# Residual with a per-sample weight matrix on one core: later bias tiles made inside the groups, the load list first in the plan, early stores issued by GpSimd, ten row slots

## The chip, the cores and the metric

The kernel runs on one core of one Trainium2 chip. The metric is the device time of one execution in microseconds (us), as the median over runs. Engines are called TensorE (PE, with its weight loads PEld), VectorE (DVE), ScalarE (ACT), GpSimd (POOL) and SyncE (SP). The last one only issues transfers and waits.

## What is computed

```python
# x [128, 64, 256] f32, cat [128] int32 in 0..63, W [64, 256, 256] f32, b [64, 256] f32
selected_W = W[cat]
selected_b = b[cat]
out = x + jnp.einsum('bsd,bdh->bsh', x, selected_W) + selected_b[:, None, :]
```

The categories of the samples are drawn once from a fixed seed. Of 64 categories 54 occur. Counted in the order in which the 128 samples meet them, the groups of eight samples need, from the first group on, the first 8, 14, 20, 26, 32, 33, 38, 41, 44, 47, 48, 52, 53, 53, 53 and 54 of the weight matrices.

## The kernel before

**Tiling.** 128 samples are 16 groups of 8. A group is 4 pairs; two pairs are a quad and share one PSUM bank of `mm_ps` (4 banks). One weight matrix is 256 KB. `w_all` has room for all 64, in the order of first use. Rows of x (512 KB a group) lie in `rows`, which has X_SLOTS = 9 slots; the sum is added in place there and stored from there, so a load of group g + 9 waits for the stores of group g.

**Plan.** The order of loads is worked out on the chip. DVE and PE make from the categories a list of categories in order of first use (`load_words`, announced by `plan_read` 1) and the slot of each sample (`slot_words`, `plan_read` 2). The steps are counted in `plan_step`, the products in `plan_products`. DVE runs its steps in program order: `same` (L362) and `in_category` (L364) stand ahead of `has_place` (L372), which the list needs, and `place_powers` (L375) stands ahead of the copy of the list (L378).

**Bias.** The bias row of each sample comes from an f32 product of a one-hot matrix with the bias table (`bias_of_tile`, one for each of 4 tiles of 32 samples). DVE splits it into three bf16 parts (`split_bias`, five instructions), and for every pair PE first writes those parts to PSUM (L508). Tile 0 is made before the first transposes, tiles 1 to 3 right after the transposes of group 0 (L467 to L470). ACT then copies them to `bias_of` (L314, L315), and DVE splits tile t at the end of its loop over group t - 1.

**Group loop on PE.** `group(g)` transposes the rows of group g + 1 (L436, 8 matmuls), writes the bias parts (L508, 8) and then does 32 matmuls (L522), four at a time waiting in pairs of `w_slot` copies. DVE copies even weights from `w_all` to `w_slot` and ACT the odd ones (L281); each copy waits for the reports of loads (`w_loads_done`). DVE adds the sums to `rows` (L405).

**Loads and stores.** The first 8 matrices are loaded by SP and ACT (one before the list exists), all others by GpSimd in the order of the list, at most 8 in flight (L256). The rows of groups 2 to 15 are loaded by GpSimd too, after the loads named in `X_AFTER_LOAD`. GpSimd begins when REPORTED_FIRST = 3 loads are reported (L246), loads group 2's rows, then reads the first word of the list (L250). For every fourth load it reads a new word. Loads from the 40th on are made only if the list is that long; a load left out still takes its turn and is reported.
SP waits for the loads in order and reports each (L204). Between the reports it issues the stores of groups 0 to 6, after the report numbers of `STORE_AFTER_REPORTS` (14, 20, 27, 35, 43, 51, 59); the stores of groups 7 to 14 come behind the 64th report. A store of a group is two transfers of 256 KB (`store_quad`), each after a wait for its sum.

Of the kernel before, what the change touches and what calls it, by code (L numbers as in the profile page):

```python
# [14 lines left out]
PAIR = 2  # L15
X_SLOTS = 9
XT_SLOTS = 2
# [4 lines left out]
FIRST_LOADS = 8  # L22
REPORTED_FIRST = 3
CERTAIN_LOADS = 40
# [6 lines left out]

PLAN_STEPS = {"samples": 6, "first": 9, "bias": 13, "list": 14, "slots": 16}

X_AFTER_LOAD = {3: 13, 4: 19, 5: 24, 6: 29, 7: 33, 8: 37, 9: 40, 10: 43, 11: 46, 12: 48, 13: 50, 14: 55, 15: 60}
STORE_AFTER_REPORTS = {0: 14, 1: 20, 2: 27, 3: 35, 4: 43, 5: 51, 6: 59}


def build_cond_residual(nc, x, cat, weights, bias, out):  # L40
# [18 lines left out]
    assert FIRST_LOADS == PAIR * WORD  # L59
    assert all(at >= min(C, GROUP * (g + 1) + QUAD - 1) for g, at in STORE_AFTER_REPORTS.items())  # L60
    assert all(X_AFTER_LOAD[g + X_SLOTS] + 1 >= STORE_AFTER_REPORTS[g] for g in range(GROUPS - X_SLOTS))

# [4 lines left out]
    with ExitStack() as ctx:  # L67
# [38 lines left out]
        bias_parts = sb("bias_parts", [ROWS, TILES, H], BF16)  # L106
        bias_of = sb("bias_of", [ROWS, TILES - 1, H])
        bias_rest = sb("bias_rest", [ROWS, H])
# [14 lines left out]
        loads_ps = mm_ps[1][0:1, 0, LIST_WORDS:LIST_WORDS + 1]  # L123
        bias_ps = [mm_ps[r][0:ROWS, n, :] for r, n in ((2, 0), (1, 1), (3, 0), (3, 1))]

# [6 lines left out]
        plan_read = sem("plan_read")  # L132
        bias_copied = sem("bias_copied")
        bias_step = sem("bias_step")
# [4 lines left out]
        x_loaded = [sem(f"x_loaded{n}") for n in range(GROUPS)]  # L139
        stored = [sem(f"stored{n}") for n in range(X_SLOTS)]  # L140
        last_stored = sem("last_stored")
        halves_transposed = sem("halves_transposed")
# [39 lines left out]
        @block.sync  # L182
        def _(sp):
            sp.dma_start(cat_row_i[:, :], cat.partition_broadcast(P)).then_inc(cats_loaded, 16)
            load_rows(sp, 0)
            sp.dma_start(bias_nat[:, :], bias).then_inc(bias_loaded, 16)

            sp.wait_ge(cats_loaded, 32)
            for g in range(1, FIRST_X):
                load_rows(sp, g)  # L190

            sp.wait_ge(plan_read, 1)
            for n in range(1, FIRST_LOADS, PAIR):
                if n % WORD == 1:
                    word = words_read(mybir.EngineType.SP, load_words[0:1, n // WORD:n // WORD + 1],
                                      2 ** (WORD * BITS) - 1)[0]
                load_weights(sp, n, part(word, n % WORD))
            for n in range(C):

                if n < FIRST_LOADS:  # L200
                    sp.wait_ge(first_w_loaded[n], 16)
                else:
                    sp.wait_ge(w_loaded[n % LOADS_IN_FLIGHT], 16 * ((n - FIRST_LOADS) // LOADS_IN_FLIGHT + 1))
                sp.sem_inc(w_loads_done, 1)  # L204
                for g, after in STORE_AFTER_REPORTS.items():
                    if after == n + 1:
                        for q in range(QUADS_IN_GROUP * g, QUADS_IN_GROUP * (g + 1)):

                            sp.wait_ge(sums_added, q + 1)
                            store_quad(sp, q, stored[g % X_SLOTS])  # L210
            for q in range(QUADS_IN_GROUP * len(STORE_AFTER_REPORTS), last_group):

                sp.wait_ge(sums_added, q + 1)
                store_quad(sp, q, stored[q // QUADS_IN_GROUP % X_SLOTS])
            for p in range(0, PAIRS_IN_GROUP, PAIR):

                sp.wait_ge(sums_added, last_group + p + 1)
                store_pair(sp, p, last_stored)

            for g in range(GROUPS - X_SLOTS - 1, GROUPS - 1):  # L220
                sp.wait_ge(stored[g % X_SLOTS], stores_until(g))
            sp.wait_ge(last_stored, 16 * PAIRS_IN_GROUP)

        @block.gpsimd
        def _(pool):
# [15 lines left out]
            pool.iota(iota_part[:, :], [[0, 1]], base=0, channel_multiplier=1,  # L241
                      allow_small_or_imprecise_dtypes=True).then_inc(consts_ready, 1)

            pool.wait_ge(plan_read, 1)

            pool.wait_ge(w_loads_done, REPORTED_FIRST)  # L246
            load_rows(pool, FIRST_X)
            for n in range(FIRST_LOADS, C):
                if n % WORD == 0:
                    word = words_read(mybir.EngineType.Pool, load_words[0:1, n // WORD:n // WORD + 1],  # L250
                                      2 ** (WORD * BITS) - 1)[0]
# [10 lines left out]
                for g, after in X_AFTER_LOAD.items():  # L262
                    if after == n:
                        if g >= X_SLOTS:

                            pool.wait_ge(stored[g % X_SLOTS], stores_until(g - X_SLOTS))
                        load_rows(pool, g)

        def slots_of(engine, g, half):
# [15 lines left out]
        def _(act):  # L285
# [25 lines left out]
            slots = slots_of(mybir.EngineType.Activation, 0, 1)  # L311

            act.wait_ge(plan_products, 5)
            nc.scalar.copy(bias_of[:, 0, :], bias_ps[1]).then_inc(bias_copied, 1)  # L314
            nc.scalar.copy(bias_of[:, 1:TILES - 1, :], mm_ps[3][0:ROWS, :, :]).then_inc(bias_copied, 1)  # L315
            for g in range(GROUPS):
# [15 lines left out]
        def _(dve):  # L332
# [9 lines left out]
            for n in range(WORD):  # L342
# [18 lines left out]
            V.tensor_scalar(cat_powers[:, :], powers[:, :], cat_col[:, 0:1], None, ALU.mult).then_inc(plan_step, 1)  # L361
            V.tensor_scalar(same[:, :], cat_row_i[:, :], cat_col[:, 0:1], None, ALU.is_equal).then_inc(plan_step, 1)  # L362
            dve.wait_ge(consts_ready, 5)
            V.tensor_scalar(in_category[:, :, :, :], cat_row_i[0:C, :].rearrange("c (t n) -> c t n", n=TILE)  # L364
                            .unsqueeze(2).broadcast_to([C, TILES, SPLITS, TILE]),
                            iota_part[0:C, 0:1], None, ALU.is_equal).then_inc(plan_step, 1)
            steps[0] += 4
            assert steps[0] == PLAN_STEPS["bias"]


            dve.wait_ge(plan_products, 1)
            step(V.tensor_scalar(has_place[:, :], iota_far[:, :], place_ps, None, ALU.is_equal))  # L372
            assert steps[0] == PLAN_STEPS["list"]
            step(V.tensor_scalar(place[:, :], place_ps, FAR, first_here[:, 0:1], ALU.add, ALU.mult))
            step(V.tensor_scalar(place_powers[:, :], powers[:, :], place[:, 0:1], None, ALU.mult))  # L375
            assert steps[0] == PLAN_STEPS["slots"]
            dve.wait_ge(plan_products, 2)
            V.tensor_copy(load_words[:, :], mm_ps[1][0:1, 0, 0:LIST_WORDS + 1]).then_inc(plan_read, 1)  # L378
            dve.wait_ge(plan_products, 3)
            V.tensor_copy(slot_words[:, :], slot_words_ps).then_inc(plan_read, 1)  # L380
# [29 lines left out]
            for g in range(GROUPS - 1):  # L410

                now, slots = slots, slots_of(mybir.EngineType.DVE, g + 2, 0) if g + 2 < GROUPS else None
                for n in range(QUADS_IN_GROUP):
                    q = QUADS_IN_GROUP * g + n

                    dve.wait_ge(pairs_done, PAIR * (q + 1))
                    add_rows(rows[:, g % X_SLOTS, PAIR * n:PAIR * (n + 1), :], mm_ps[q % BANKS][:, :, :])
                    for p in range(PAIR * n, PAIR * n + PAIR):
                        copy_weights(dve, V.tensor_copy, now[p], g + 1, p, 0, even_weights_ready)
                if g + 1 < TILES:  # L420

                    dve.wait_ge(bias_copied, 2)
                    dve.wait_ge(bias_ready, PAIR * (g + 1))
                    split_bias(g + 1, bias_of[:, g, :])
            for p in range(PAIRS_IN_GROUP):
# [5 lines left out]
        def _(pe):  # L431
# [26 lines left out]
            last.then_inc(plan_products, 1)  # L458

            pe.wait_ge(bias_loaded, 16)  # L460
            bias_of_tile(0).then_inc(plan_products, 1)

            pe.wait_ge(x_loaded[0], 16)
            for k in range(K):
                transpose_half(0, k)

            pe.wait_ge(plan_read, 1)  # L467
            for t in range(1, TILES):
                last = bias_of_tile(t)
            last.then_inc(plan_products, 1)  # L470

            def group(g):
# [17 lines left out]

                pe.wait_ge(xT_ready, K * (g + 1))
                if g == 0:

                    pe.wait_ge(bias_ready, PAIR)

                    pe.wait_ge(bias_copied, 2)
                if PAIRS_IN_GROUP * g % PAIRS_IN_TILE == 0:

                    pe.wait_ge(bias_ready, PAIR * (PAIRS_IN_GROUP * g // PAIRS_IN_TILE + 1))
                for pair in range(PAIRS_IN_GROUP):  # L500
# [49 lines left out]
```

## Time and profile before

| what | value |
|---|---|
| median of 3 runs | 106.52 us (105.53 to 107.8) |
| profiled execution, its own time | 107.0 us |
| span of the profiled execution | 105.3 us |
| PE busy | 90.7 us (86% of the span) |
| DVE, ACT, GpSimd busy | 56.2, 56.3, 45.8 us |
| moved by DMA | 31.26 MB, 297 GB/s over the span |

The span runs from the first to the last instruction. Busy time is time with an instruction in work on that engine. A share of the span is an average over stages with different limits, so the stages have to be looked at one by one. The granted clock of TensorE is given as a share of full speed (2.4 GHz), so 0.5 is 1.2 GHz. The DMA share is the mean busy share of the 16 DMA engines.

### The profile page before, as it was taken

How to read it: one execution, taken by the hardware profiler on the slowest of the kernel's cores; microseconds unless marked ns; L12 is line 12 of the kernel's file. 1: busy time of each engine (PE TensorE's matmuls, PEld its weight loads, DVE VectorE, ACT ScalarE, POOL GpSimd, SP SyncE). 2: the span in 40 equal slices, each digit the busy share in tenths (PEclk: the TensorE clock that was granted, in tenths of full speed). 3: DMA queues.
4: the chain of work that ended last, by engine and by line, in shares of the span. 5: the costliest groups of instructions: out<-in, count | busy, mean ns of one | idle time of the engine just before them, and what ended most of it. 6: DMA issues, size and time to landing. Idle time of an engine off the chain costs nothing.

```text
span 105.3 us, 3045 instructions
## 1 busy us (share of the span) xinstructions
PE 90.7 (86%) x786; PEld 60.5 (57%) x786; DVE 56.2 (53%) x137; ACT 56.3 (53%) x99; POOL 45.8 (43%) x81
## 2 busy tenths in 40 slices
PE   0039999999958838999999999999999999999960
PEld 0026576656626517557576767666766767676630
DVE  1086403558848696175547473829282828364740
ACT  0000866556324618279766666667585858584400
POOL 5000078977888889867678353005503011000000
PEclk9999999999999998599999999999999999999999
DMA  0576998999999999999999999926883805999994
GB/s 10 150 266 170 345 340 274 356 325 339 377 396 351 389 402 361 353 401 387 364 363 398 406 361 375 403 90 120 254 332 120 280 11 184 330 343 326 305 344 168
DMA packets 18049, 31.26 MB, mean 297 GB/s; under 512 B 1840, under 2 KB 13296, under 8 KB 18032
## 3 DMA queue, kind: packets, MB, share of 16 engines
q0 software_dynamic: 5696, 19.40, 51.5%
q1 hardware_dynamic: 10816, 10.36, 29.3%
q10 hardware_dynamic: 1520, 1.31, 4.4%
q8 instruction: 6, 0.10, 0.4%
q14 instruction: 11, 0.09, 0.2%
HBM read 25.30 MB, written 8.39 MB: 320 GB/s over the span
## 4 chain that ended last, share of the span: by engine, by line
PE 59%; DMA 14%; issue 11%; POOLq 4%; POOL 4%; DVE 3%; ACT 1%; SPq 1%; ACTq 0%
PE mm_ps L522 39%; PE xt_ps L436 11%; DMA w_all<-in_L_cond_W 10%; PE mm_ps L508 6%; DMA cat_col_i<-in_itok_B 4%; POOL w_all L159 3%; POOLq L153 2%; POOLq L159 2%; PE xt_ps L522 2%; POOL rows L168 1%; ACT w_slot L281 1%; DVE rows L405 0%; DVE same_ahead L354 0%; SPq L153 0%; DVE in_category L364 0%
## 5 line engine op out<-in xcount | busy, mean ns | idle before, releaser
L522 PE MATMUL mm_ps<-w_slot,xT 128*64 128x256 f32 x496 | 58.5, 385 | 4.0 <-ACT w_slot L281 3.9
L281 ACT COPY w_slot<-w_all 128x512 f32 x64 | 39.0, 620 | 31.4 <-SPq L204 16.5
L522 PEld LDWEIGHTS mm_ps<-w_slot,xT 128*64 128x64 f32 x496 | 35.4, 140 | 22.0 <-issue 6.2
L159 POOL DMA_DIRECT2D w_all<-in_L_cond_W x56 | 33.2, 595 | 14.8 <-issue 7.3
L405 DVE TENSOR_TENSOR rows<-mm_ps,rows 128x512 f32<-128x512 f32 (+1 forms) x32 | 21.5, 673 | 25.3 <-PE mm_ps L522 24.5
L281 DVE COPY w_slot<-w_all 128x512 f32 x64 | 26.7, 446 | 13.4 <-SPq L204 13.3
L168 POOL DMA_DIRECT2D rows<-in_x x14 | 10.9, 781 | 26.4 <-DMA out<-rows 16.1
L436 PE MATMUL xt_ps<-ident,rows 128*128 128x128 f32 x128 | 19.9, 304 | 0.1
L436 PEld LDWEIGHTS xt_ps<-ident,rows 128*128 128x128 f32 x128 | 15.6, 154 | 7.0 <-issue 6.0
L293 ACT COPY xT<-xt_ps 128x512 f32<-128x512 f32 x32 | 17.1, 584 | 0.0
L508 PE MATMUL mm_ps<-bias_parts,is_sample 96*64 96x256 bf16 x124 | 10.8, 297 | 0.0
L508 PEld LDWEIGHTS mm_ps<-bias_parts,is_sample 96*64 96x64 bf16 x124 | 6.0, 115 | 3.1 <-issue 2.8
L293 ACT ACT_TABLE_LOAD x1 | 1.3, 1283 | 10.6 <-issue 10.6
L447 PE MATMUL mm_ps<-is_first,ahead_or_self 128*128 128x1 bf16 x1 | 0.2, 183 | 5.8 <-DVE is_first L357 5.8
L442 PE MATMUL mm_ps<-bias_nat,in_category 64*96 64x256 f32 x8 | 4.0, 658 | 0.0
L447 PEld LDWEIGHTS mm_ps<-is_first,ahead_or_self 128*128 128x128 bf16 x1 | 0.1, 102 | 5.8 <-DVE is_first L357 5.8
L442 PEld LDWEIGHTS mm_ps<-bias_nat,in_category 64*96 64x96 f32 x8 | 1.9, 268 | 1.0 <-issue 0.3
L522 PE MATMUL xt_ps<-w_slot,xT 128*64 128x256 f32 x16 | 2.1, 379 | 0.0
L351 DVE CAST cat_col<-cat_col_i 128x1 f32<-128x1 int32 x1 | 0.2, 155 | 3.1 <-DMA cat_col_i<-in_itok_B 3.1
L398 DVE TENSOR_TENSOR bias_parts<-bias_rest,bias_mid 32x256 bf16<-32x256 f32 x4 | 1.7, 417 | 0.1
L522 PEld LDWEIGHTS xt_ps<-w_slot,xT 128*64 128x64 f32 x16 | 1.1, 137 | 0.6
L395 DVE TENSOR_TENSOR bias_rest<-bias_of,bias_parts 96x256 f32<-96x256 f32 x3 | 1.3, 422 | 0.1
(42 smaller groups left out, 13.1 us busy)
## 6 DMA issues: line engine op xcount, KB each, us to landing
w_all<-in_L_cond_W POOLq DMA_DIRECT2D x56, 256.0 KB
out<-rows SPq DMA_DIRECT2D x30, 256.0 KB, 4.1
rows<-in_x POOLq DMA_DIRECT2D x14, 512.0 KB, 7.6
rows<-in_x SPq DMA_DIRECT2D x2, 512.0 KB, 4.6
w_all<-in_L_cond_W ACTq DMA_DIRECT2D x4, 256.0 KB, 4.8
w_all<-in_L_cond_W SPq DMA_DIRECT2D x4, 256.0 KB, 6.1
out<-rows SPq DMA_DIRECT2D x2, 128.0 KB, 2.9
out<-rows ACTq DMA_DIRECT2D x2, 128.0 KB, 2.9
```

What stands on the lines that cost most here:

```text
L153: return nc.values_load_multi_w_load_instructions(words, engines=[engine], min_val=0, max_val=most)[1]
L159: engine.dma_start(w_all[:, n, :, :], weights[bass.ds(c, 1), :, :].rearrange("c (k p) h -> p (c k) h", p=P), **how).then_inc(first_w_loade ...
L168: engine.dma_start(rows[:, g % X_SLOTS, :, :], x_groups[g]).then_inc(x_loaded[g], 16)
L281: copy(w_slot[:, PAIR * p + half, :, :].rearrange("p k h -> p (k h)"), w_all[:, bass.ds(c, 1), :, :].rearrange("p c k h -> p (c k h)")).th ...
L293: nc.scalar.copy(xT[:, slot, k].rearrange("p j s -> p (j s)"), xt_ps[slot][k][:, :, :].rearrange("p t r -> p (t r)")).then_inc(xT_ready, 1)
L395: split(V.tensor_tensor(bias_rest[all3, :], whole, bias_parts[all3, t, :], ALU.subtract))
L398: V.tensor_tensor(bias_parts[third, t, :], bias_rest[third, :], bias_mid[third, :], ALU.subtract).then_inc(bias_ready, 1)
L405: V.tensor_tensor(to, sums, to, ALU.add).then_inc(sums_added, 1)
L436: last = T.transpose(xt_ps[g % XT_SLOTS][k][:, p, :], rows[:, g % X_SLOTS, p, k * P:(k + 1) * P], ident[:, :])
L442: return T.matmul(bias_ps[t], in_category[:, t, :, :].rearrange("c a n -> c (a n)"), bias_nat[:, :], start=True, stop=True)
L508: T.matmul(sums(pair)[HALF * half:HALF * (half + 1), :], is_sample[:, sample + half:sample + half + 1].broadcast_to([ROWS, HALF]), bias_pa ...
L522: last = T.matmul(to[HALF * half:HALF * (half + 1), :], xT[:, slot, k, j, :], w_slot[:, j, k, :], start=False, stop=(k == K - 1), skip_gro ...
```

## The change

`PLAN_STEPS` is put into a new order: DVE makes `has_place`, `place` and the copy of the list before `same`, `place_powers` and `in_category`. Tiles 1 to 3 of the bias are no longer made ahead of group 0: PE makes tile g in `group(g)`, behind its transposes, in a bank of `mm_ps` that has just come free, and DVE splits it straight from PSUM at the start of its loop over group g. The copies on ACT and `bias_of` are gone. GpSimd reads its first list word before it waits for the reports, and waits for five of them, not three. GpSimd also issues the stores of groups 0 to 10: those of groups 0 to 6 behind loads 33, 37, 40, 43, 46, 51 and 59, the rest after its last load. SP stores groups 11 to 15. There are ten row slots.

```diff
-X_SLOTS = 9
+X_SLOTS = 10
-REPORTED_FIRST = 3
+REPORTED_FIRST = 5
-PLAN_STEPS = {"samples": 6, "first": 9, "bias": 13, "list": 14, "slots": 16}
+PLAN_STEPS = {"samples": 6, "first": 9, "list": 12, "slots": 15, "bias": 16}
-X_AFTER_LOAD = {3: 13, 4: 19, 5: 24, 6: 29, 7: 33, 8: 37, 9: 40, 10: 43, 11: 46, 12: 48, 13: 50, 14: 55, 15: 60}
-STORE_AFTER_REPORTS = {0: 14, 1: 20, 2: 27, 3: 35, 4: 43, 5: 51, 6: 59}
+X_AFTER_LOAD = {3: 13, 4: 19, 5: 24, 6: 29, 7: 33, 8: 37, 9: 40, 10: 43, 11: 46, 12: 48, 13: 51, 14: 55, 15: 60}
+STORE_AFTER_LOAD = {0: 33, 1: 37, 2: 40, 3: 43, 4: 46, 5: 51, 6: 59}
+POOL_GROUPS = 11
...
-        bias_ps = [mm_ps[r][0:ROWS, n, :] for r, n in ((2, 0), (1, 1), (3, 0), (3, 1))]
+        bias_ps = [mm_ps[r % BANKS][0:ROWS, 0, :] for r in (2, 4, 6, 8)]
...
 # SP
-                for g, after in STORE_AFTER_REPORTS.items():
-                    if after == n + 1:
-                        for q in range(QUADS_IN_GROUP * g, QUADS_IN_GROUP * (g + 1)):
-                            sp.wait_ge(sums_added, q + 1)
-                            store_quad(sp, q, stored[g % X_SLOTS])
-            for q in range(QUADS_IN_GROUP * len(STORE_AFTER_REPORTS), last_group):
+            for q in range(QUADS_IN_GROUP * POOL_GROUPS, last_group):
                 sp.wait_ge(sums_added, q + 1)
-                store_quad(sp, q, stored[q // QUADS_IN_GROUP % X_SLOTS])
+                store_quad(sp, q, late_stored)
...
 # GpSimd
+            def store_group(g):
+                for q in range(QUADS_IN_GROUP * g, QUADS_IN_GROUP * (g + 1)):
+                    pool.wait_ge(sums_added, q + 1)
+                    store_quad(pool, q, stored[g % X_SLOTS])
             pool.wait_ge(plan_read, 1)
+            word = words_read(mybir.EngineType.Pool, load_words[0:1, FIRST_LOADS // WORD:FIRST_LOADS // WORD + 1],
+                              2 ** (WORD * BITS) - 1)[0]
             pool.wait_ge(w_loads_done, REPORTED_FIRST)
             load_rows(pool, FIRST_X)
...
+                for g, after in STORE_AFTER_LOAD.items():
+                    if after == n:
+                        store_group(g)
+            for g in range(len(STORE_AFTER_LOAD), POOL_GROUPS):
+                store_group(g)
...
 # ACT
-            act.wait_ge(plan_products, 5)
-            nc.scalar.copy(bias_of[:, 0, :], bias_ps[1]).then_inc(bias_copied, 1)
-            nc.scalar.copy(bias_of[:, 1:TILES - 1, :], mm_ps[3][0:ROWS, :, :]).then_inc(bias_copied, 1)
...
 # DVE, in its loop over g
+                if 1 <= g < TILES:
+                    dve.wait_ge(tiles_made, g)
+                    dve.wait_ge(bias_ready, PAIR * g)
+                    split_bias(g, bias_ps[g])
                 for n in range(QUADS_IN_GROUP):
...
-                if g + 1 < TILES:
-                    dve.wait_ge(bias_copied, 2)
-                    dve.wait_ge(bias_ready, PAIR * (g + 1))
-                    split_bias(g + 1, bias_of[:, g, :])
...
 # PE
-            pe.wait_ge(plan_read, 1)
-            for t in range(1, TILES):
-                last = bias_of_tile(t)
-            last.then_inc(plan_products, 1)
...
                 pe.wait_ge(xT_ready, K * (g + 1))
+                if 1 <= g < TILES:
+                    pe.wait_ge(sums_added, QUADS_IN_GROUP * (g - 1) + 1)
+                    bias_of_tile(g).then_inc(tiles_made, 1)
                 if g == 0:
                     pe.wait_ge(bias_ready, PAIR)
-                    pe.wait_ge(bias_copied, 2)
-                if PAIRS_IN_GROUP * g % PAIRS_IN_TILE == 0:
-                    pe.wait_ge(bias_ready, PAIR * (PAIRS_IN_GROUP * g // PAIRS_IN_TILE + 1))
+                elif 1 < g <= TILES:
+                    pe.wait_ge(bias_ready, PAIR * g)
```

## Rows read from the trace of the kernel before

**Rows 1.** Page, part 2: granted TensorE clock in 40 equal slices, in tenths.

```profile
PEclk9999999999999998599999999999999999999999
```

**Rows 2.** Chain that ended last, in order of time: start us, us, what.

```profile
31.68 7.19 DMA w_all<-in_L_cond_W
...
47.52 1.03 PE xt_ps L436 x8
48.54 0.56 PE mm_ps L508 x8
49.10 3.46 PE mm_ps L522 x32
```

**Rows 3.** Timeline of PE, 25 to 48 us: start, us, instruction, [idle before <-releaser].

```profile
31.93 1.08 PE L522 MATMUL mm_ps<-w_slot,xT 128*64 128x256 f32 x8 [1.52 <-ACT w_slot L281]
...
39.77 1.08 PE L522 MATMUL mm_ps<-w_slot,xT 128*64 128x256 f32 x8 [1.87 <-ACT w_slot L281]
...
43.28 4.23 PE L522 MATMUL mm_ps<-w_slot,xT 128*64 128x256 f32 x32
```

**Rows 4.** Busy time by stretch: PE, PEld, DVE, ACT, POOL, PEclk, DMA share, GB/s.

```profile
24.00:38.90 14.90, 11.64 (x103) 7.47 (x99) 11.10 (x27) 6.04 (x11) 12.19 (x18) 1.00 1.03 376
...
30.00:40.80 10.80, 6.91 (x61) 4.32 (x57) 7.91 (x19) 5.13 (x10) 9.09 (x13) 1.00 1.04 382
40.80:44.60 3.80, 3.80 (x26) 2.79 (x26) 1.43 (x4) 1.46 (x3) 3.46 (x6) 0.55 1.02 347
```

**Rows 5.** Reports of loads (L204), six stretches from 0: count, ns, first to last.

```profile
L204 SPq EVENT_SEMAPHORE  x3: 17/17/17, 11.9 to 12.3; - x3
...
L204 SPq EVENT_SEMAPHORE  x5: 17/17/17, 11.9 to 15.6; - x5
...
L204 SPq EVENT_SEMAPHORE  x8: 17/17/17, 11.9 to 17.6; - x8
...
L204 SPq EVENT_SEMAPHORE  x26: 17/17/17, 11.9 to 38.9; - x26
...
L204 SPq EVENT_SEMAPHORE  x32: 17/17/17, 11.9 to 45.3; - x32
...
L204 SPq EVENT_SEMAPHORE  x47: 17/17/17, 11.9 to 64.7; - x47
```

**Rows 6.** Timeline of GpSimd, 12 to 46 us.

```profile
13.01 0.89 POOL L168 DMA_DIRECT2D rows<-in_x  x1 [10.24 <-SPq L204]
14.54 2.86 POOL L159 DMA_DIRECT2D w_all<-in_L_cond_W  x4 [0.64 <-issue]
17.91 1.43 POOL L159 DMA_DIRECT2D w_all<-in_L_cond_W  x2 [0.51 <-issue]
```

**Rows 7.** Timeline of all engines, 0 to 22 us: plan and bias tiles.

```profile
6.53 0.25 DVE L372 TENSOR_SCALAR has_place<-iota_far,mm_ps 128x64 bf16<-128x64 f32 x1
...
7.32 0.17 DVE L378 CAST load_words<-mm_ps 1x17 int32<-1x17 f32 x1
...
10.55 2.87 PE L442 MATMUL mm_ps<-bias_nat,in_category 64*96 64x256 f32 x6
```

**Rows 8.** Issues by line, stores in two stretches: count, ns, first to last; landing.

```profile
L159 POOL DMA_DIRECT2D w_all<-in_L_cond_W x56: 44/706/795, 14.5 to 88.0; - x56
...
DMA to landing us min/median/max: 3.2/6.0/6.2
...
L168 POOL DMA_DIRECT2D rows<-in_x x14: 748/776/892, 13.0 to 86.4; - x14
...
L172 SPq DMA_DIRECT2D out<-rows x2: 393/448/502, 23.5 to 23.9; - x2
...
L172 SPq DMA_DIRECT2D out<-rows x2: 373/422/472, 31.1 to 31.5; - x2
...
DMA to landing us min/median/max: 7.0/8.3/9.7
```

**Rows 9.** Waits, longest first: us in total, times, longest us.

```profile
POOL rows L168 <- DMA out<-rows: 16.1, 4, 7.1
```

More of the change, by code:

```diff
@@ L59, in build_cond_residual @@
     assert FIRST_LOADS == PAIR * WORD
-    assert all(at >= min(C, GROUP * (g + 1) + QUAD - 1) for g, at in STORE_AFTER_REPORTS.items())
-    assert all(X_AFTER_LOAD[g + X_SLOTS] + 1 >= STORE_AFTER_REPORTS[g] for g in range(GROUPS - X_SLOTS))
+    assert all(at + 1 >= min(C, GROUP * (g + 1) + QUAD - 1) for g, at in STORE_AFTER_LOAD.items())
+    assert all(X_AFTER_LOAD[g + X_SLOTS] >= STORE_AFTER_LOAD[g] for g in range(GROUPS - X_SLOTS))
     x_groups = x.rearrange("(g p h) s d -> g (h s) p d", p=PAIRS_IN_GROUP, h=PAIR)
@@ L106, in build_cond_residual @@
         bias_parts = sb("bias_parts", [ROWS, TILES, H], BF16)
-        bias_of = sb("bias_of", [ROWS, TILES - 1, H])
         bias_rest = sb("bias_rest", [ROWS, H])
@@ L132, in build_cond_residual @@
         plan_read = sem("plan_read")
-        bias_copied = sem("bias_copied")
+        tiles_made = sem("tiles_made")
         bias_step = sem("bias_step")
@@ L140, in build_cond_residual @@
         stored = [sem(f"stored{n}") for n in range(X_SLOTS)]
+        late_stored = sem("late_stored")
         last_stored = sem("last_stored")
@@ L218, in _ @@
                 store_pair(sp, p, last_stored)
-            for g in range(GROUPS - X_SLOTS - 1, GROUPS - 1):
+            for g in range(POOL_GROUPS - X_SLOTS, POOL_GROUPS):
                 sp.wait_ge(stored[g % X_SLOTS], stores_until(g))
+            sp.wait_ge(late_stored, 16 * (last_group - QUADS_IN_GROUP * POOL_GROUPS))
             sp.wait_ge(last_stored, 16 * PAIRS_IN_GROUP)
@@ L248, in _ @@
             for n in range(FIRST_LOADS, C):
-                if n % WORD == 0:
+                if n % WORD == 0 and n > FIRST_LOADS:
                     word = words_read(mybir.EngineType.Pool, load_words[0:1, n // WORD:n // WORD + 1],
@@ L361, in _ @@
             V.tensor_scalar(cat_powers[:, :], powers[:, :], cat_col[:, 0:1], None, ALU.mult).then_inc(plan_step, 1)
-            V.tensor_scalar(same[:, :], cat_row_i[:, :], cat_col[:, 0:1], None, ALU.is_equal).then_inc(plan_step, 1)
+            steps[0] += 2
             dve.wait_ge(consts_ready, 5)
[L364 to L368, printed above, removed]
             dve.wait_ge(plan_products, 1)
@@ L374, in _ @@
             step(V.tensor_scalar(place[:, :], place_ps, FAR, first_here[:, 0:1], ALU.add, ALU.mult))
-            step(V.tensor_scalar(place_powers[:, :], powers[:, :], place[:, 0:1], None, ALU.mult))
-            assert steps[0] == PLAN_STEPS["slots"]
             dve.wait_ge(plan_products, 2)
             V.tensor_copy(load_words[:, :], mm_ps[1][0:1, 0, 0:LIST_WORDS + 1]).then_inc(plan_read, 1)
+            V.tensor_scalar(same[:, :], cat_row_i[:, :], cat_col[:, 0:1], None, ALU.is_equal).then_inc(plan_step, 1)
+            V.tensor_scalar(place_powers[:, :], powers[:, :], place[:, 0:1], None, ALU.mult).then_inc(plan_step, 1)
+            steps[0] += 2
+            assert steps[0] == PLAN_STEPS["slots"]
+            V.tensor_scalar(in_category[:, :, :, :], cat_row_i[0:C, :].rearrange("c (t n) -> c t n", n=TILE)
+                            .unsqueeze(2).broadcast_to([C, TILES, SPLITS, TILE]),
+                            iota_part[0:C, 0:1], None, ALU.is_equal).then_inc(plan_step, 1)
+            steps[0] += 1
+            assert steps[0] == PLAN_STEPS["bias"]
             dve.wait_ge(plan_products, 3)
@@ L458, in _ @@
             last.then_inc(plan_products, 1)
+            pe.wait_ge(plan_step, PLAN_STEPS["bias"])
             pe.wait_ge(bias_loaded, 16)
```

## The prediction

> **What bounds the kernel now.** Read the clock by slices first, then the chain of work that ended last, then the idle times on PE's timeline. The chain shows two regimes. From about 40.9 us to the end it lies on PE, in groups that repeat: 1.03 us of transposes, 0.56 of bias parts, 3.46 of products, 5.05 us together [rows 2]. Nothing waits there. Before that, the chain runs along GpSimd's issues and ends in the landing of the 26th weight load: issued at 31.68, landed 7.19 us later [rows 2]. The report comes at 38.9 [rows 5], ACT copies the matrix, and PE's last eight products of group 3 start at 39.77 after 1.87 us of idleness; in group 2 the same place had 1.52 us [rows 3]. From 30 to 40.8 us PE is busy for 6.91 of 10.80 us, while the DMA engines are full (share 1.04, 382 GB/s) [rows 4]. So groups 1 to 3 are paced by the supply of weights, groups 4 to 15 by PE. After that poor stretch the clock falls: its mean is 0.55 from 40.8 to 44.6 [rows 4], and the dip to 0.8 and 0.5 is the only one in the slices [rows 1]. That is the lower level, 1.2 GHz, for most of the stretch, and group 4 lasts from 40.85 (39.77 + 1.08) to 47.52 [rows 2, 3], 6.67 us and not 5.05: 1.6 us lost.
>
> Hence the rule for this case: what moves the end of group 4 moves the end of the kernel one for one, if the later weights keep ahead of PE. What does not is hidden.
>
> **The stores moved behind the weights.** The stores of group 0 (two transfers at 23.5 and 23.9) and group 1 (31.1 and 31.5) share the full DMA engines with loads 15 to 26 [rows 8]. The latter pair lands up to 9.7 us after its issue, to 41.2, so of the four transfers of 0.262 MB about 3.5 are moved before 38.9: 0.92 MB. At 376 GB/s, the rate from 24 to 38.9 us [rows 4], that is 2.4 us. The changed kernel issues its first store after the 34th load, so report 26 gains these 2.4 us as far as the transfers set it.
>
> **The list earlier.** `has_place` starts at 6.53 because it stands behind `in_category`; the copy of the list starts at 7.32, behind `place_powers` [rows 7]. With those behind it, `has_place` can start when `in_category` would have, some 0.4 us sooner, and the list gains about 0.15 us more since `place_powers` no longer stands ahead of its copy: 0.55 us. The bounds are 0.2 and the 0.8 us between the two starts. The first eight loads start that much earlier. The slots and bias tile 0 come 0.1 to 0.2 us later; hidden, since group 0 waits for weights.
>
> **GpSimd starts later.** Three reports are there at 12.3, five at 15.6, all eight at 17.6 [rows 5]. GpSimd's rows load, now queued behind the fifth report, was issued at 13.01, 0.7 us after the third, and its first weights at 14.54 [rows 6]. In the changed kernel the fifth report comes earlier: 0.55 us for the list, and about 0.65 us because the 0.52 MB of rows issued at 13.01 no longer share the engines then (about 0.2 MB of it by 15.6, at the rate above). That is 14.4. The word of the list is already read, so the first weights follow 0.7 + 0.9 us after: 16.0, 1.4 us later than now. Bounds: 0, if the fifth report came right behind the third, and 2.1 us with no relief but the list's (15.6 - 0.55 + 1.6 - 14.54). Everything GpSimd issues is behind this wait: the rows of group 2, then all loads.
>
> GpSimd's own pace then matters. From its first weights to the 26th load (index 25) there are 17 loads of 0.706 us (12.0), three rows loads of 0.776 (2.3) [rows 8] and four word reads at 0.5 [rows 6] (2.0): 16.3 us, where it took 17.1 now (31.68 - 14.54). So the 26th load is issued at 32.4, 0.7 later than now. Landing: a load takes 3.2 us at least, 6.0 in the median, this one 7.19 [rows 2, 8]. With no store between I take 4.3, near the lower end, since the eight first loads are through before GpSimd's come: report 26 at 36.7 (35.6 to 38.4). By the transfers: 38.9 - 2.4 - 0.55, and plus about 1.0 us for a gap in the DMA stream while GpSimd waits, gives 36.95. The two ways agree; I take 36.7, **2.2 us earlier**.
>
> **Group 4.** From report 26 to the end of group 3 it takes 2.0 us now (38.9 to 40.85 [rows 3, 5]), so group 3 ends at 38.7. Report 32 follows after six loads and one rows load, 2.1 MB, 5.6 us at 376 GB/s: 42.3 (45.3 now, with stores in between [rows 5]). Its copy and products put the end of group 4 at 44.3 or later; PE alone would need 38.7 + 5.05 = 43.75 at full clock. So 44.3 against 47.52: **3.2 us**. The clock's 1.6 us is in this, with 0.55 us of it spent on the wait for report 32. I count the clock as staying at 2.4 GHz since PE's idleness in groups 2 and 3 shrinks: each group has now about 6.4 us for 5.5 us of work, where it was busy for 64% of the stretch from 30 to 40.8.
>
> **The bias tiles.** Three tiles took PE 2.87 us at the low clock ahead of group 1's transposes [rows 7]. They go to groups 1 to 3, 0.96 us each at the low and about 0.48 at the full clock. In groups 1 to 3 the last weights are later than PE's other work, so 0.5 us a group is covered (without the cover, were PE to bound there, 1.4 us in all). Group 0 gets the 2.87 us back, but weights and clock pace it: counted 0. DVE now waits in groups 1 to 3 for PE's tile before it can split; behind that wait stand the sum of the group's first quad and the even copies of the next group, which are not due for some 3 us. PE's next user of that sum is two groups on: 0. ACT loses two copies, ahead of odd weights that mostly have not landed: 0 to 0.3 us, I take 0.
>
> **Stores on GpSimd.** No row shows a store issued there. The nearest below is the same transfer on SP (0.37 to 0.50 us to issue), the nearest above the same 256 KB as a load on GpSimd, 0.706, at most 0.795, and a rows load at up to 0.892 [rows 8]. I take 0.71, the same size and row length. Eight of them (groups 0 to 3) stand ahead of the 47th load: 5.7 us. By issue alone, from 32.4 on with 21 loads (14.8), five rows loads (3.9), five word reads (2.5) and these, the 47th goes out at 32.4 + 26.9 = 59.3 and lands by 63.6; by transfers, 21 loads, five rows loads and four groups of stores after report 26, 10.2 MB at 376 GB/s, it is 27.2 us after 36.7: report 47 at 63.9, 64.7 now [rows 5]. Group 9, whose last pair needs it, ends near 44.3 + 5 x 5.05 = 69.6, and wants the report by 67.6. So 3.7 us to spare, and more for the other groups. Each such store also waits for its sum, with loads queued behind it; the sums are long there (group 3's at about 39, its store near 56).
>
> The Trainium skill, page "SBUF — State Buffer", section "SBUF: two separate sides", has a rule that speaks against this edit: DVE's f32 copies inside SBUF lock GpSimd out while it makes descriptors. It gives 620 ns alone and 3100 ns beside such a copy, by which the eight stores would cost up to 20 us more. This trace does not agree: of 56 issues, with DVE's even copies running between them, none took over 795 ns [rows 8]. The sum goes by that row.
>
> **Ten slots, SP at the end.** GpSimd waits 16.1 us in four places for stores before rows loads [rows 9]; these are off the chain. With ten slots and the stores queued well ahead the waits go; what becomes free is time on GpSimd, worth nothing at the end. The stores of groups 7 to 10 leave before the tail, so the last stores meet emptier engines: 0 to 0.3 us, I take 0.1.
>
> **Sum.** 3.2 + 0.1 = 3.3 us. 107.0 - 3.3 = 103.7 for the profiled execution; the median shown is 0.5 us lower than that execution, so **103.2 us**.
>
> **The rivals.**
> 1. *The clock falls all the same*, or stays at the low level through group 1. For it: gaps in groups 2 and 3 remain. Against it: they are halved. Cost 1.6 less the 0.55 us that group 4 waits anyway: 1.0, so 104.2. Chance 0.13.
> 2. *Issue, not transfer, sets the supply.* If landing stays at the 6.0 median or more, report 26 comes at 38.4 or later, and little is gained: the chain of before does run along GpSimd from 13 to 31.7 us, and it now starts later. Against it: engines full at 1.04. Time 105.3 to 106.5, say 105.9. Chance 0.13.
> 3. *More is gained*: with earlier first weights and no stores, PE bounds from group 0 on. It can't end group 4 before about 19 + 3 x 5.5 + 5.05 = 40.6, a gain of 6.9 (19 is my estimate for the end of group 0: eighth report at 17.6 - 0.55 - 1.2, plus 3 us for the last two pairs at the low clock). Time 99.6 to 101.7, say 101.2. Chance 0.10.
> 4. *Slower: stores issued by GpSimd make later weights late.* The 3.7 us to spare at load 47 are gone in transfers; on the issue side (63.6 against 67.6) eight stores may each cost 0.5 us more, 1.21 us. Beyond that point each further 0.1 us costs 0.8 us, and the gain of 3.3 is used up at 1.6 us a store. At 2.0 us each: 103.2 + 8 x (2.0 - 1.21) = 109.5, slower than before. The lock named above would work so. Against it: the 795 ns. Chance 0.05.
>
> **How the numbers follow.** The forecast holds 0.59, its own range 101.9 to 104.4 (report 26 from 35.8 to 38.0). With rivals 1 and 3 in part and 2 in part, 101.0 to 105.6 leaves out 0.2: half of rivals 2 and 3, rival 4 and a little more. About 2% can be told from no change, so faster is under 104.4: the forecast nearly whole (0.56), rival 3 (0.10), over half of rival 1 (0.08): 0.74. Within 2%: 0.21. Slower: 0.05.
>
> **What would show it.** Right: no store before load 34; report 26 between 36 and 37.5; clock 1.0 from 36 to 46 us; group 4 over by 44.5; from there groups of 5.05; GpSimd's stores at 0.7 us; no wait for `out` before rows loads. Wrong: the first GpSimd weights after 16.7, a store over 1.2 us, groups past the fourth longer than 5.1 us, or a wait of PE for rows of group 2, issued 2 us later than now.

## The result, and the profile after

| kernel | median us | ratio to the kernel before | 95% interval |
|---|---|---|---|
| before | 106.59 | 1 | |
| changed | 105.37 | 0.9882 | 0.9846 to 0.9919 |

The change takes 1.2 us off, not 3.3. The time lies within the range that was given, near its upper end; the gain is about a third of the forecast. A second measurement gave less still: a ratio of 0.994 (0.990 to 0.999). Here and below the medians count every execution, while the ratios leave out the slow ones, those over 1.5% longer than the fastest of their kernel, of which the profiled execution of the kernel before with five reports is one (110.82 us). The profiled execution of the changed kernel took 105.33 us with a span of 103.6, so its span is 1.7 us shorter. I follow these 1.7 us.

First the granted clock and the flow of data by slices, page, part 2, of the changed kernel:

```profile
PEclk9999999999999999999999999999999999999999
DMA  0587994999999999999999999999997799993353
GB/s 10 143 273 220 291 314 167 334 324 331 354 332 350 353 347 345 348 356 399 351 391 372 394 367 400 373 388 350 373 392 271 227 333 320 331 322 114 108 202 105
```

The dip of the clock [rows 1] is gone. But two things stand in the GB/s row: a hole (167) at 15.5 to 18 us, with a DMA share of 0.4, and then a flat stretch near 350 up to 44 us, where the kernel before had 376 to 382 up to 40.8 us [rows 4] with stores among its loads.

The reports of loads (L207 of the changed kernel), counted from 0, answer to [rows 5]:

```profile
L207 SPq EVENT_SEMAPHORE  x5: 17/17/17, 11.3 to 14.8; - x5
...
L207 SPq EVENT_SEMAPHORE  x14: 17/17/17, 11.3 to 24.9; - x14
...
L207 SPq EVENT_SEMAPHORE  x26: 17/17/17, 11.3 to 38.6; - x26
...
L207 SPq EVENT_SEMAPHORE  x32: 17/17/17, 11.3 to 44.6; - x32
...
L207 SPq EVENT_SEMAPHORE  x64: 17/17/17, 11.3 to 81.0; - x64
```

Of the kernel before, these are the two that [rows 5] does not have:

```profile
L204 SPq EVENT_SEMAPHORE  x14: 17/17/17, 11.9 to 23.4; - x14
...
L204 SPq EVENT_SEMAPHORE  x64: 17/17/17, 11.9 to 88.0; - x64
```

Report 14 is 1.5 us later than before, report 26 only 0.3 us earlier and report 32 0.7 us. So the supply lost 1.5 us at its start, won it back, and won hardly more. The timeline of GpSimd answers to [rows 6]:

```profile
15.13 0.90 POOL L171 DMA_DIRECT2D rows<-in_x  x1 [12.37 <-SPq L207]
16.03 2.82 POOL L162 DMA_DIRECT2D w_all<-in_L_cond_W  x4
...
32.12 2.11 POOL L162 DMA_DIRECT2D w_all<-in_L_cond_W  x3
```

The 26th load (index 25) is the first of the three from 32.12 on. The timeline of PE answers to [rows 3]:

```profile
28.86 0.64 PE L450 MATMUL mm_ps<-bias_nat,in_category 64*96 64x256 f32 x2 [0.79 <-DVE rows L413]
...
39.48 1.08 PE L527 MATMUL mm_ps<-w_slot,xT 128*64 128x256 f32 x8 [1.20 <-ACT w_slot L292]
...
45.51 1.08 PE L527 MATMUL mm_ps<-w_slot,xT 128*64 128x256 f32 x8 [0.76 <-ACT w_slot L292]
```

In the chain that ended last, the landing from which it passes to PE is now that of the 32nd load:

```profile
37.38 7.22 DMA w_all<-in_L_cond_W
```

Group 4 ends at 46.59 (45.51 + 1.08) and not at 47.52, 0.93 us earlier. It runs at full clock, and part of what the clock gives back it spends waiting for its last weights (0.76 us). From there the groups take 5.04 us each, as before, and the last sum comes 0.93 us earlier too. The remaining 0.8 us of the span are at the very end. The last stores of pairs, from issue to landing, in the kernel before and then in the changed one:

```profile
DMA to landing us min/median/max: 2.6/2.9/3.3
```

```profile
DMA to landing us min/median/max: 1.7/1.7/1.8
```

### The profile page after: what moved, and what is told of

The parts are those of the page before. It is cut to its first block, busy times and chain, and to the rows that moved or that the text cites. A ratio compares the mean times of both kernels' runs of the same rounds, so it can differ in the third digit from the quotient of the medians.

```text
span 103.6 us, 3047 instructions
## 1 busy us (share of the span) xinstructions
PE 87.4 (84%) x786; PEld 58.2 (56%) x786; DVE 57.0 (55%) x137; ACT 55.0 (53%) x97; POOL 62.0 (60%) x103
## 3 DMA queue, kind: packets, MB, share of 16 engines
q1 hardware_dynamic: 4832, 4.59, 13.5%
## 4 chain that ended last, share of the span: by engine, by line
PE 54%; DMA 16%; issue 15%; POOL 6%; POOLq 3%; DVE 2%; ACT 1%; ACTq 0%; SPq 0%; DVEq 0%
PE mm_ps L527 36%; DMA w_all<-in_L_cond_W 12%; PE xt_ps L444 10%; PE mm_ps L513 6%; POOL w_all L162 5%; DMA cat_col_i<-in_itok_B 4%; POOLq L162 2%; PE xt_ps L527 2%; POOL rows L171 1%; POOLq L156 1%; ACT w_slot L292 1%; DVE rows L413 0%; DVE same_ahead L361 0%; DVE has_place L373 0%; PE mm_ps L458 0%
## 5 line engine op out<-in xcount | busy, mean ns | idle before, releaser
L527 PE MATMUL mm_ps<-w_slot,xT 128*64 128x256 f32 x496 | 57.8, 380 | 5.3 <-ACT w_slot L292 4.0
L527 PEld LDWEIGHTS mm_ps<-w_slot,xT 128*64 128x64 f32 x496 | 34.5, 137 | 22.9 <-issue 4.9
L413 DVE TENSOR_TENSOR rows<-mm_ps,rows 128x512 f32<-128x512 f32 (+1 forms) x32 | 21.6, 674 | 23.9 <-PE mm_ps L527 23.0
L444 PE MATMUL xt_ps<-ident,rows 128*128 128x128 f32 x128 | 19.0, 298 | 0.4 <-DMA rows<-in_x 0.4
L171 POOL DMA_DIRECT2D rows<-in_x x14 | 11.0, 786 | 13.5 <-SPq L207 12.9
L175 POOL DMA_DIRECT2D out<-rows x22 | 16.1, 736 | 1.1 <-issue 1.1
L513 PE MATMUL mm_ps<-bias_parts,is_sample 96*64 96x256 bf16 x124 | 9.9, 278 | 0.1
L450 PE MATMUL mm_ps<-bias_nat,in_category 64*96 64x256 f32 x8 | 3.1, 478 | 0.8 <-DVE rows L413 0.8
L402 DVE CAST bias_parts<-mm_ps 96x256 bf16<-96x256 f32 x4 | 1.7, 420 | 1.9 <-PE mm_ps L450 1.0
L450 PEld LDWEIGHTS mm_ps<-bias_nat,in_category 64*96 64x96 f32 x8 | 1.1, 182 | 1.5 <-issue 1.3
L403 DVE TENSOR_TENSOR bias_rest<-mm_ps,bias_parts 96x256 f32<-96x256 f32 x4 | 1.7, 420 | 0.1
```

The source lines that it names most:

```text
L171: engine.dma_start(rows[:, g % X_SLOTS, :, :], x_groups[g]).then_inc(x_loaded[g], 16)
L175: engine.dma_start(out_pairs[:, PAIR * q:PAIR * (q + 1), :], rows[:, g % X_SLOTS, PAIR * n:PAIR * (n + 1), :]).then_inc(done, 16)
L402: split(V.tensor_copy(bias_parts[all3, t, :], whole))
L403: split(V.tensor_tensor(bias_rest[all3, :], whole, bias_parts[all3, t, :], ALU.subtract))
L413: V.tensor_tensor(to, sums, to, ALU.add).then_inc(sums_added, 1)
L444: last = T.transpose(xt_ps[g % XT_SLOTS][k][:, p, :], rows[:, g % X_SLOTS, p, k * P:(k + 1) * P], ident[:, :])
```

## The experiments

All ratios are to the kernel before as run in the same comparison; there were four (106.59, 106.60, 106.13 and 106.41 us). "Group 4 ends" is the start of group 5's transposes in the chain of the profile, or the end of group 4's products on PE's timeline. The row "before, five reports" comes from an execution 1.7 us longer than the median of its kernel, so its three times are too late by an unknown part of that.

| run | median us | ratio, 95% interval | report 14 | report 26 | group 4 ends |
|---|---|---|---|---|---|
| before | 106.59 | 1 | 23.4 | 38.9 | 47.5 |
| before, five reports | 109.14 | 1.022 (1.016 to 1.028) | 26.3 | 42.9 | 51.5 |
| before, no early stores | 104.47 | 0.979 (0.972 to 0.985) | 23.1 | 37.9 | 45.8 |
| before, ten slots | 105.97 | 0.999 (0.995 to 1.003) | 23.6 | 39.5 | 48.1 |
| changed | 105.37 | 0.988 (0.985 to 0.992) | 24.9 | 38.6 | 46.6 |
| changed, again | 106.11 | 0.994 (0.990 to 0.999) | 24.8 | 39.3 | 47.3 |
| changed, all stores on SP | 107.02 | 1.006 (1.002 to 1.010) | 23.9 | 39.5 | 47.8 |
| changed, three reports | 103.76 | 0.973 (0.969 to 0.977) | 23.5 | 37.9 | 45.9 |
| the same, again | 103.96 | 0.980 (0.975 to 0.985) | 23.3 | 37.4 | 45.4 |
| changed, one report | 104.32 | 0.984 (0.980 to 0.989) | 23.2 | 37.0 | 44.9 |
| changed, three reports, all stores on SP | 105.74 | 0.995 (0.991 to 1.000) | 23.3 | 38.3 | 46.9 |
| changed, stores of 7 to 10 on SP | 105.95 | 0.997 (0.993 to 1.001) | 24.4 | 38.3 | 46.3 |
| changed, rows on SP | 109.39 | 1.032 (1.026 to 1.039) | 26.0 | 38.4 | 46.0 |
| the same, three reports | 109.60 | 1.031 (1.022 to 1.039) | 24.2 | 36.7 | 49.2 |

Two profiles of an unaltered kernel differ here by 0.7 us at report 26, so single profiles are read in pairs where that can be done.

### What the early stores cost the loads

```diff
 # the kernel before; x of groups 9 and 10 wait for the sums instead
-                    if after == n + 1:
+                    if after == n + 1 and g > 1:
```

> The kernel before, with the stores of groups 0 and 1 left out altogether (their part of the output is not written). It measures what these four transfers of 0.262 MB cost the loads. Theory 'part price': loads alone run at 349 GB/s and stores beside them raise the total, so a stored byte costs the loads only about 0.6 of a byte: report 26 at 38.9 - 1.8 = 37.1 us. Rival 'full price' (that of my prediction): 1.05 MB at 349 GB/s, report 26 at 35.9 to 36.5. Rival 'free': report 26 stays at 38.9. Of the time, part price gives 1.5 to 3 us less than the kernel before, full price 3 to 4, free none.

Report 26 came at 37.9, 1.0 us earlier. That is between free and part price: 1.05 MB at 349 GB/s would be 3.0 us, so a stored byte costs the loads about a third of a byte at report 26. By the bytes loaded it is more: from 24 to 38.9 us this kernel loaded 5.12 MB and the kernel before 4.56, which is 0.56 MB for 1.03 MB of stores. Part of that went to loads behind the 26th. The time fell by 2.1%, within the 1.5 to 3 us; group 4 ended 1.7 us earlier, more than report 26 moved, since the clock stayed up (PE's row of the clock has no dip) and report 32 came 1.4 us earlier.

The reason can be read from the busy time by stretch, 25 to 38 us. Columns are as in [rows 4]. The kernel before, with stores; then without the early ones; then the changed kernel:

```profile
25.00:38.00 13.00, 10.64 (x94) 6.69 (x90) 9.34 (x23) 5.04 (x9) 10.54 (x16) 1.00 1.04 378
```

```profile
25.00:38.00 13.00, 10.93 (x98) 7.01 (x94) 9.68 (x23) 4.68 (x9) 11.77 (x17) 1.00 1.01 347
```

```profile
25.00:38.00 13.00, 12.11 (x108) 8.03 (x108) 11.04 (x25) 6.55 (x12) 12.12 (x17) 1.00 1.02 349
```

The engines are full in all three (1.01 to 1.04). Loads alone move 347 and 349 GB/s in these 13 us, and 346 to 353 in the other kernels without early stores. With stores among them it is 378, and 368 to 377 in three of the four other kernels that store there; the fourth, the kernel before with five reports, stored half as much in the stretch (0.52 MB) and had 350. The DMA queues of the stretch from 24 to 38.9 us split this: packets, MB, share of the engines. First the kernel before, then the changed one:

```profile
q0 software_dynamic: 1358, 4.56, 82.8%
q1 hardware_dynamic: 1060, 1.03, 19.8%
```

```profile
q0 software_dynamic: 1539, 5.19, 101.6%
```

In 14.9 us the kernel before loaded 4.56 MB and stored 1.03 beside it; the changed one loaded 5.19. Taking 1.03 MB of stores away brought 0.63 MB of loads here. So a busy share of 1.0 did not mean that a byte taken away frees its whole time.

### Is it reads that are limited, or GpSimd's queue?

```diff
 # the changed kernel; SP, behind its report
+                for g, after in X_AFTER_LOAD.items():
+                    if max(after - LOADS_IN_FLIGHT + 1, 0) == n:
+                        if g >= X_SLOTS:
+                            sp.wait_ge(stored[g % X_SLOTS], stores_until(g - X_SLOTS))
+                        load_rows(sp, g)
 # GpSimd
-                        load_rows(pool, g)
```

> The changed kernel with the rows loads of groups 3 to 15 issued by SP in its report loop, as the reports of eight loads earlier come. It asks why loads alone stay at 349 GB/s. Theory 'read limit': reads are limited whatever queue they come from, so the total stays at 340 to 355 GB/s from 25 to 38 us and report 26 near 38.6. Rival 'queue limit': GpSimd's queue alone can't do more; with a quarter of the bytes on SP's queue the total rises to 376 or more, report 26 comes 1 us earlier, and the time falls by 1 us or more.

The same stretch of that kernel, then its two queues from 25 to 38 us:

```profile
25.00:38.00 13.00, 11.87 (x106) 7.70 (x104) 9.97 (x24) 7.07 (x13) 9.66 (x14) 1.00 1.05 349
```

```profile
q0 software_dynamic: 1066, 3.48, 78.6%
q1 hardware_dynamic: 1030, 1.03, 25.3%
```

Here too q1 carries 1.03 MB beside q0 (in the kernel before these were stores), and the total is 349, not 376. The changed kernel shows the other half. Its stores begin at 41 us on GpSimd's own queue, so that one queue carries loads and stores together, and from 44.6 us on the rate is higher:

```profile
44.60:60.00 15.40, 14.64 (x140) 9.97 (x140) 8.86 (x18) 11.96 (x22) 14.72 (x21) 1.00 1.03 377
```

So it is the direction and not the queue: over long stretches loads alone stay near 349 GB/s here, and stores beside them raise the sum. Nor is it GpSimd's issuing: with three reports it was busy for 10.87 and 10.70 of the 13 us, and not for 12.12, at the same 348 and 349 GB/s. The figure is no hard stop over a short time: from 15 to 20 us, with the last of the first eight loads still arriving, the two runs with three reports loaded at 355 and 363 GB/s. Why loads alone stay there was not found. Report 26 came at 38.4, as the read limit has it. The time was not the same, though: it is 3% above the kernel before and some 4% above the changed one, and all of that comes after group 4. The rows now share the engines with the weights on a queue of their own and come late (issue to landing 11.5 us in the median, 7.6 in the changed kernel). PE idled 3.6 us for them in five places, 0.4 us in the changed kernel, which is about the 3.3 us by which the span is longer:

```profile
PE xt_ps L443 <- DMA rows<-in_x: 3.6, 5, 1.0
```

> As the run with rows loads on SP, with GpSimd's start behind three reports. Read limit: the time of the changed kernel with three reports, 103.8 us, within 0.5 us. Queue limit: 102.5 to 103.0 us.

It gave 348 GB/s from 25 to 38 us and 109.6 us. The rate held, the time did not. PE idled 4.7 us for rows, 2.1 of them at 35.15 us, and here the clock fell as well, to 0.6 and 0.5 of full speed from 35 to 43 us.

### GpSimd's later start

```diff
-REPORTED_FIRST = 5
+REPORTED_FIRST = 3
```

> The changed kernel with GpSimd's start behind three reports as before instead of five. Theory 'late start': the five-report wait costs the supply 1.1 us or more, at report 14 (24.9 in the changed kernel, 23.4 before) and still at report 26: expect report 14 at 23.2 to 23.8, report 26 at 37.3, and 1.0 to 1.4 us less than the changed kernel. Rival 'caught up': loads in flight catch up by report 26; 38.6 as now, and the same time. Rival 'first loads first': the rows load in front of the first eight delays report 8 by 0.8 us and the time is not better.

> The changed kernel once more, unaltered, for a comparison on one chip with the runs with three and one reports: 105.2 to 105.5 us if the kernel before gives 106.5.

> The changed kernel with three reports once more, on the same chip as the changed kernel: 1.2 to 1.6 us less than it if the earlier comparison (0.9727 against 0.9882 of the kernel before) holds, 0.7 us less if the profile's spans (102.9 and 103.6) tell the truth.

On one chip, three reports gave 103.96 and five 106.11; in the separate comparisons 103.76 and 105.37. In ratios that is 1.4 to 1.6% or 1.5 to 1.7 us. Over two profiles each, report 14 comes at 23.4 and not 24.9, report 26 at 37.7 and not 39.0, group 4 ends at 45.7 and not 47.0: what is lost at the start is still missing at group 4. "Caught up" and "first loads first" are out (report 8 comes 0.2 to 0.4 us later, not 0.8, and the time is better). The gain is somewhat above the 1.0 to 1.4 us expected, and the changed kernel's second time is above its 105.2 to 105.5. The stretch from 15 to 20 us shows the hole and its absence, the changed kernel first, then with three reports:

```profile
15.00:20.00 5.00, 3.75 (x31) 2.56 (x32) 1.78 (x3) 3.06 (x6) 4.49 (x7) 1.00 0.70 226
```

```profile
15.00:20.00 5.00, 3.94 (x32) 2.69 (x32) 2.23 (x4) 3.21 (x6) 4.62 (x7) 1.00 1.04 355
```

The 26th load shows what binds. With three reports it was issued at 30.26 and 30.40 and not at 32.12, and landed only 0.7 and 1.2 us earlier, after 7.7 and 7.0 us and not after 6.5. Issued earlier, it waits longer.

As for the hole, 129 GB/s over 5 us are 0.65 MB, or 1.8 us at 349 GB/s; 0.2 MB of it had been moved earlier, from 10 to 15 us (311 against 272 GB/s).

> The kernel before with GpSimd's start behind five reports instead of three, nothing else. Late start: report 14 from 23.4 to 25, report 26 from 38.9 to about 40, time 1.0 to 1.5 us more than the kernel before. Caught up: report 26 and the time as before.

In the kernel before, the same single number costs 2.3 to 2.5 us (1.022), against 1.0 to 1.5 expected. Report 14 is 2.9 us later in its profiled execution, but that one was 1.7 us longer than the median. There GpSimd also reads its first word only behind the wait, the clock falls again, and the stores keep their places. How much each of these adds was not taken apart.

> The changed kernel with GpSimd's start behind one report. Late start goes on: one report is there at 11.3, some 0.9 us before the third; if the start sets the supply, report 26 comes near 37.0 and the time falls another 0.5 to 0.9 us below the one with three reports. Rival 'engines full': from 10 us on the engines are busy at 0.91 and more with three reports, so nothing is gained, and the first eight weights come up to 0.8 us later: the same time or up to 0.5 us more.

Report 26 moved on to 37.0 and the span to 101.9, but the time did not follow, as the rival had it: 0.984 against 0.980 on the same chip, intervals overlapping. Report 8 came at 18.4, 1.1 us later than with three, and group 0 ended 0.9 us later. Three reports is as good a place as any measured; it beats both kernels.

### The stores' place in the changed kernel

```diff
 # the changed kernel: SP's report loop has the old STORE_AFTER_REPORTS,
 # POOL_GROUPS = 7, and GpSimd stores nothing
-                for g, after in STORE_AFTER_LOAD.items():
-                    if after == n:
-                        store_group(g)
-            for g in range(len(STORE_AFTER_LOAD), POOL_GROUPS):
-                store_group(g)
```

> The changed kernel with all stores on SP as before (groups 0 to 6 behind reports 14, 20, 27, 35, 43, 51, 59, the others behind the 64th). Only the plan, the bias tiles, the five reports and ten slots of the change are left. Part price: report 26 at 38.6 + 1.8 = 40.4 and group 4 ends 1.5 to 2 us later than in the changed kernel, time 1.5 to 2.5 us more than it, that is slightly more than the kernel before. Full price: report 26 at 41.6, 3 us more. Free: report 26 at 38.6, and the time of the changed kernel plus at most 0.8 us at the tail.

> The changed kernel with all stores on SP at the old points and GpSimd's start behind three reports: what is left of the change is the list ahead of the other steps, the bias tiles in the groups, the word read ahead of the wait, and ten slots. It was 107.0 us with five reports. Late start: five reports cost here what they cost the changed kernel (1.0 to 1.6 us) or up to what they cost the kernel before (2.5), so 104.5 to 106.0, report 26 at 38.0 to 38.8. If the plan part is worth nothing: 106.6, as the kernel before.

With five reports, the old places cost 1.2 to 1.8% (1.006 against 0.988 and 0.994 of the kernel before), 1.3 to 1.9 us. Group 4 ends 1.2 us later and report 26 comes 0.9 later than in the first profile of the changed kernel, 0.5 and 0.2 later than in its second. With three reports it is 1.5 to 2.2% (0.995 against 0.980 and 0.973); over the two profiles with three reports, group 4 ends 1.3 us later and report 26 comes 0.6 later. The time is what part price said or somewhat less, report 26 is between part price and free (39.5, where part price had 40.4). Group 4 moved more than report 26 did, for two reasons. With three reports and the old places the clock falls again and group 4 takes 6.7 us (40.26 to 46.92), with the late stores 6.0 (39.88 to 45.92). With five reports the clock stays up, but the stores of group 2 stand among the next loads, and report 32 comes at 45.8 and not at 44.6 or 45.4. What is left of the change there, the plan, the bias tiles, the early word and ten slots, is worth 0.5% (0.0 to 0.9).

### The tail

```diff
-POOL_GROUPS = 11
+POOL_GROUPS = 7
```

> The changed kernel with the stores of groups 7 to 10 on SP behind the 64th report, as before, the early ones still on GpSimd. Theory 'clear tail': the last pair stores landed after 1.7 us in the changed kernel and 2.9 in the one before, because stores no longer pile up behind the 64th report; with the pile back the time rises by about 0.7 us and the last landing goes back to 2.5 to 3 us. Rival: the pile is through before the last pairs (the 64th report comes at 81, not at 88), so nothing changes.

> The kernel before with ten row slots (and the rows of group 13 after load 51), nothing else. Theory 'ten slots clear the tail': the rows loads no longer wait long for stores, the 64th report comes near 80 and not 88, the stores behind it are gone before the end, and the last ones land after 1.7 us and not 2.9: 0.7 to 0.9 us less than the kernel before, group 4 ending as there (47.5). Rival 'tail worth nothing': same time. Third: the plan part and not the tail made the 1.4 us of span between the plan-and-bias run and the kernel before; then this run stays at the span of before, 105.3.

With the stores of groups 7 to 10 back on SP the last ones still land after 1.7 us: the pile is gone as long as the 64th report comes at 80. In the kernel before, ten slots alone bring it to 79.1, and the last stores land in 1.8 us:

```profile
L204 SPq EVENT_SEMAPHORE  x64: 17/17/17, 11.9 to 79.1; - x64
```

```profile
DMA to landing us min/median/max: 1.7/1.8/1.8
```

So the 0.8 us at the end of the span belong to the tenth slot, not to who issues the stores. They did not show as a gain of their own, though: the ratio is 0.999. In that profile report 26 came 0.6 us and group 4's end 0.5 us later than in the kernel before, which eats most of the 0.8; whether that is chance or comes with the slot was not tried (the profiled execution was 0.8 us longer than the median of its kernel). The run with the late stores on SP, at 0.997, lies above the changed kernel's 0.988 but about where its second measurement is; the profile shows no cost (group 4 ends at 46.3). Whether the tail of 0.8 us is worth 0.8 us of time stays unclear by these.

## Why the prediction fell short, step by step

**What bounds the kernel: right in the main.** The chain still passes through weight landings, the last now that of load 32, and lies on PE from group 5 on. What moved the end of group 4 moved the last sum: 0.93 us both.

**The list earlier: right.** Its copy starts at 6.80 and not 7.32, 0.52 us.

**GpSimd's start and pace: right as times of issue, wrong in what they cost.** Fifth report 14.8 (14.4 foreseen), first weights 16.03 (16.0), the 26th load 32.12 (32.4). But it landed after 6.5 us and not after 4.3. This is the step that failed: **the landing of the 26th load**, sized 2.2 us too short, as much as the whole gain that I had put at report 26. No row supported 4.3: the median was 6.0 and this load had taken 7.19. Two things were wrong in it. The check by transfers used 376 GB/s for a stretch from which the stores had been taken, although the 376 held the stores: 4.72 MB from report 14 to 26 at 376 are 12.6 us, at the 349 that loads alone reach 13.5; measured 13.7. And the hole in the DMA stream, put at 1.0 us with 0.55 of the list against it, left report 14 1.5 us late, not 0.45. The two ways to report 26 agreed by luck: one had a landing that was too short, the other a rate that was too high and a hole that was too small. The rest of the sum held. Report 26 came 1.9 us later than foreseen, the 2.1 MB to report 32 took 6.0 us and not 5.6, again 349 and not 376 GB/s, and from report 32 to the end of group 4 it was 2.0 us as foreseen: together the 2.3 us by which group 4 is late (46.6, not 44.3).

**The stores moved: right sign, price two to four times too high.** 2.4 us foreseen for report 26; leaving them out altogether brings 1.0 us, moving them 0.6 in the pair with three reports. Rival 2 (issue, not transfer) had the number of report 26, 38.4 or later, and also the time (105.3 to 106.5), but not the cause: issuing was on time, an earlier issue brought less than its own time, and reading was the limit. Its chance was put at 0.13.

**Group 4 and the clock: right in mechanism, hidden.** The clock stays at its high level, as foreseen, and group 4 still needed 6.0 us since report 32 came at 44.6, not 42.3. Its 1.6 us were counted in full less 0.55; 0.6 us came of them (6.67 to 6.03). Rival 1, the clock falling all the same, did not occur in the changed kernel.

**The bias tiles: a wait that I had put at 0.** PE's next user of group 1's first sum is not two groups on, as the prediction has it: it is the bias tile of group 2. There PE waits 0.79 us for the sum of a quad that DVE adds only after it has split the tile before (28.86 above). It is covered here, since group 3 then waits for report 26 anyway. With a faster supply it could be the next thing late; no run shows that.

**Rows of group 2: a sign of being wrong that appeared.** PE waited 0.36 us for them before their transposes at 19.28, 0.19 us in the second profile. It is hidden, since PE waits 1.02 us for weights in the same group.

**Stores on GpSimd: right.** 0.71 us each foreseen; the line of the changed kernel:

```profile
L175 POOL DMA_DIRECT2D out<-rows x22: 707/723/815, 41.0 to 86.7; - x22
```

Rival 4 is out. The Trainium skill, page "SBUF — State Buffer", section "SBUF: two separate sides", gives 3100 ns for a transfer issued by GpSimd beside a DVE copy. This trace does not agree: no store took over 815 ns, and the two from 55.36 to 56.88 us, with two DVE copies running between 55.59 and 56.39, took 0.76 us each. Report 47 came at 66.5, not 63.9: 1.9 us of it from the late report 26, the rest on the way from there. It was wanted by 69.9 (group 9 ends at 71.8), so the reserve was 3.4 us, as foreseen (3.7).

**Ten slots and the tail: undersized.** 0.1 us foreseen, 0.8 in the span.

In sum, 2.2 us were expected from report 26 and 0.3 came; 3.2 from group 4 and 0.93 came; 0.1 from the tail and 0.8 came. With three reports instead of five, the change gives 2.0 to 2.7% rather than 0.6 to 1.2: the number forecast for the change, 103.2, is nearly reached by a version without its late start (103.8 and 104.0).

## What to carry to other kernels

A busy share of 1.0 on the DMA engines does not say what a byte is worth: read the GB/s of a stretch with the same mix of loads and stores as the stretch that is forecast, and if there is none, bound the rate by the stretches of loads alone. When a whole stream hangs on one engine's first issue, a wait ahead of it can be paid nearly in full where that stream is the limit: here 1.4 us at report 14 and 1.3 at the end of group 4. A gain in clock or in compute that ends before the next due load is not a gain yet; compute the next arrival before adding it.

## What the runs showed of the hardware

I had not expected that loads alone stay at 346 to 353 GB/s over 13 us, whether one queue carries them or two, at a busy share of 1.01 to 1.05, while loads and stores together reach 368 to 378 with the engines showing as just as full, on one queue or two. Nor that four stores, put among loads, cost so little of their own time: 1.0 us at report 26 for 1.05 MB, and 0.56 MB of loads for 1.03 MB of stores.
